# A three-sublayer model on 4096 tokens: projection, scan, router and first mixture as one pipeline over blocks of 512 tokens

## The reference, cut to what matters

```python
# scan, per sequence; x_in = x @ w_in, (dt_low, B, C) = split(x_in @ w_x)
dt = softplus(dt_low @ w_dt + b_dt) * (DT_MAX - DT_MIN) + DT_MIN
A = -exp(A_log)                       # 128 channels x 16 states
def step(h, inp):
    dA = dtt[:, :, None] * A
    h = exp(dA) * h + einsum('bdn,bn,bd->bn', dA, bt, ut)[:, None, :]
    y = einsum('bdn,bn->bd', h, ct) + Dp * ut
# mixture over N = 4096 tokens, 8 experts, capacity C = 512
logits = x @ Wr + br
probs = softmax(logits); gate = max(probs); idx = argmax(probs)
mask = one_hot(idx); pos = cumsum(mask, axis=0) * mask
mask = mask * (pos < C)               # the tokens behind the 511th of an expert are dropped
gate = gate * sum(mask)
combine = gate * one_hot(idx) x one_hot(pos)
expert_in = einsum('nd,nec->ecd', x, combine)
h = relu(expert_in @ W1[e] + b1[e]); eo = h @ W2[e] + b2[e]
out = einsum('ecd,nec->nd', eo, combine)
```

## Time and profile before

| | us |
|---|---|
| median of 3 runs | 571.65 |
| span of the profiled execution | 585.5 |
| PE busy | 312.8 |
| DVE busy | 362.3 |
| ACT busy | 224.5 |
| POOL busy | 306.3 |

### The profile page before, as it was taken

One profiled execution on the slowest core, in us unless ns is written; L12 is line 12 of the kernel. 1 busy time (PEld: TensorE's weight loads), 2 busy tenths in 40 slices (PEclk: granted clock), 3 DMA queues, 4 the chain that ended last, 5 costly groups with the idle time before them and its releaser, 6 DMA issues.

```text
span 585.5 us, 5360 instructions
## 1 busy us (share of the span) xinstructions
PE 312.8 (53%) x1281; PEld 160.1 (27%) x1281; DVE 362.3 (62%) x801; ACT 224.5 (38%) x350; POOL 306.3 (52%) x225
## 2 busy tenths in 40 slices
PE   4878343666657657565150826054787464073700
PEld 3333110111111112145140513022575453042400
DVE  4484689999999999976250202195689964011204
ACT  2768854355354354214140302056546022120303
POOL 3041155777686677745655366337224855627550
PEclk9988775787787787875555868559989575567655
DMA  7003429500000000020104421430000000143019
GB/s 194 0 1 107 161 58 319 219 0 1 0 0 0 0 0 0 0 57 27 50 33 123 134 81 40 118 93 1 1 1 6 32 33 28 50 137 107 36 66 266
DMA packets 34996, 37.74 MB, mean 64 GB/s; under 512 B 5529, under 2 KB 27035, under 8 KB 34972
## 3 DMA queue, kind: packets, MB, share of 16 engines
q1 hardware_dynamic: 30076, 28.34, 16.4%
q0 software_dynamic: 4096, 8.43, 4.0%
q10 hardware_dynamic: 800, 0.71, 0.4%
HBM read 17.47 MB, written 19.99 MB: 64 GB/s over the span
## 4 chain that ended last, share of the span: by engine, by line
issue 34%; PE 6%; POOL 4%; another core or an unknown queue 4%; SPq 3%; DMA 3%; ACT 1%; DVE 0%; POOLq 0%; ACTq 0%; DVEq 0%
POOL answers L1063 4%; PE ps L989 2%; PE ps L998 2%; DMA back<-answers 1%; PE ps L980 1%; SPq L1147 1%; SPq L1080 1%; SPq L949 1%; DMA rows<-slots 1%; DMA answers<-reply,home 1%; ACT rows_t L1018 0%; ACT back L1089 0%; ACT hidden L1024 0%; DVE reply L1052 0%
## 5 line engine op out<-in xcount | busy, mean ns | idle before, releaser
L643 POOL TENSOR_TENSOR states<-states,c_rows 128x1024 f32<-128x1024 f32 x44 | 119.1, 2709 | 51.0 <-DVE states L663 50.8
L663 DVE TENSOR_TENSOR_SCAN states<-ps,inp 128x1024 f32<-128x1024 f32 x64 | 142.2, 2268 | 2.6 <-ACT ps L628 2.6
L628 ACT ACTIVATE ps<-ps,bias_p,scale_p 128x1024 f32<-128x1024 f32 x64 | 74.4, 1176 | 88.4 <-PE ps L566 88.4
L1063 POOL DMA_INDIRECT answers<-reply,home x64 | 61.4, 959 | 51.3 <-DVE reply L1052 33.3
L566 PE MATMUL ps<-stack,sel 96*128 (+1 forms) x128 | 49.3, 486 | 69.2 <-DVE states L663 63.2
L890 POOL DMA_INDIRECT slots<-gated,put x64 | 63.5, 993 | 42.4 <-ACT gated L882 24.7
L1052 DVE TENSOR_TENSOR reply<-ps,b 128x512 f32 x16 | 11.1, 691 | 67.3 <-PE ps L998 45.3
L577 PE MATMUL ps<-states,red 128*32 128x512 f32 x256 | 46.0, 813 | 2.3 <-POOL states L643 2.3
L566 PEld LDWEIGHTS ps<-stack,sel 96*128 96x128 bf16 x128 | 9.0, 104 | 122.3 <-DVE states L663 89.1
L733 POOL TENSOR_TENSOR rstd<-spread,neg_half 128x8 f32<-128x8 f32 x12 | 20.8, 1736 | 32.1 <-DVE neg_mean L727 32.1
L989 PE MATMUL ps<-rows_t,e_w 128*128 128x512 f32 x32 | 23.1, 812 | 19.2 <-ACT rows_t L1018 19.2
(11 more groups left out here) (160 smaller groups left out, 607.2 us busy)
## 6 DMA issues: line engine op xcount, KB each, us to landing
slots<-zero SPq DMA_DIRECT2D x8, 516.0 KB
rows<-slots SPq DMA_DIRECT2D x16, 258.0 KB, 2.7
back<-answers SPq DMA_DIRECT2D x8, 512.0 KB, 6.1
steps<-part SPq DMA_DIRECT2D x4, 768.0 KB, 3.2
stack<-steps SPq DMA_DIRECT2D x12, 256.0 KB, 4.0
x<-in_x SPq DMA_DIRECT2D x4, 512.0 KB, 5.8
answers<-zero SPq DMA_DIRECT2D x4, 512.0 KB
e_w<-in_f_W SPq DMA_DIRECT2D x16, 128.0 KB
```

Of the source, the lines that this page charges most:

```text
L628: act.activation(slot(u), slot(u), ACT.Exp, scale=m["scale_p"][:, group(u):group(u) + 1], bias=m["bias_p"][:, group(u):group(u) + 1]).then ...
L643: eng.tensor_tensor(h[:, u * SEQ:(u + 1) * SEQ], h[:, u * SEQ:(u + 1) * SEQ], c_rows[:, bass.ds(b * SEQ, SEQ)], ALU.mult).then_inc(done, 1)
L663: dve.tensor_tensor_scan(h[:, u * SEQ:(u + 1) * SEQ], slot(u), inp[:, bass.ds(b * SEQ, SEQ)], 0.0, ALU.mult, ALU.add).then_inc(scanned, 1)
L1063: pool.indirect_dma_start(out=m["answers"], out_offset=bass.IndirectOffsetOnAxis(m["home"][:, e, j:j + 1], 0), in_=m["reply"][:, e, j * D: ...
```

## The change

Both plans stay, but the first now holds everything up to the first mixture in one function, `stream`, and the second (`conv_and_mixture`) starts with the statistics for the convolution. The unit is a block of 512 tokens (8 blocks); the scan of a sequence's second block starts from the last states of the first. All engines run through one list of steps, 16 steps (channel groups) to a block, and each piece of work has a fixed place in it: the constants give the step, counted from the block's first scan, at which a piece is issued. Buffers for two blocks take the place of those for all sequences; the scan's buffer in PSUM becomes three single banks.

The layer norm moves: the mean is taken out by the matrix `center` folded into the weights, and the normalization for the router is applied to the logits. The residual x and the scan's output are summed in PSUM (`state_sum`), go out transposed (`xt`), back to tokens (`back`, `take_x`), and feed the logits. All products with C are on POOL.

The first mixture computes all 8 experts for all tokens: a first layer (`first`) from the transposed block, and a second bf16 matmul onto it, from 56 features per token, which adds the bias and a term of -1e30 for each expert that wasn't chosen, so that its Relu gives zero; the second layers (`second`) of all experts sum up in one bank, and `mix` adds the result, weighted by gate and capacity, into x. The weight of expert layers stays in SBUF for the second mixture. The convolution's filter and its weights are prepared inside the steps (`prepare`, steps 1 to 20). The first block's step sizes are broadcast by fp32 matmuls, without the way over DRAM. The second mixture is as before, with its two loops written out. `need` now issues no wait where the count is zero.

```diff
-            project(plan, ps, m, t)
-            scan(plan, ps, m, t)
+            stream(plan, ps, m, t)
...
+DECAY, Y_BANK, TURN_BANK, PROJ_BANK, HIDDEN_BANK, OUT_BANK = 0, 3, 4, 5, 6, 7
+AHEAD = 2
+LAG = 3
+RING = 12
+STATS_IN, POW_IN, NORMAL_IN, TOKENS_IN = -20, -19, -18, -17
+Z_AT, U_AT, B_AT, C_AT, Q_AT = -16, -15, -14, -13, -11
+SOFTPLUS, DTU, HIGH, REST, MIDDLE, LOW, INPUT = -13, -12, -12, -11, -10, -9, -10
+SUMS = QUARTERS - 1 + LAG
+TAKE_Y, BACK, TAKE_X, LOGITS, STATS_X, POW_X, CHOOSE, PROB, COUNT, PLACE, FEATURES, WEIGH = 19, 19, 20, 20, 21, 22, 23, 24, 24, 25, 26, 27
+MIX = 27
+FIRST_STEP, LAST_STEP = STATS_IN, GROUPS * (BLOCKS - 1) + MIX + 2 * EXPERTS + 3
...
+        def clear(dst, b):
+            wide = dst.shape[1]
+            sp.dma_start(dst[b * SEQ:(b + 1) * SEQ, :].rearrange("(p j) d -> p (j d)", p=P), zero[:, 0:BT * wide]).then_inc(prepared, 16)
+        def spread_steps(k):
+            need(sp, low_done, k)
+            sp.dma_start(m["steps"][:, k * PARTS * HALF:(k + 1) * PARTS * HALF], part[:, :, :].rearrange("p a s -> p (a s)")).then_inc(steps_out, 16)
+            sp.wait_ge(steps_out, k * 16)
+            need(sp, dt_psum, GROUPS * (k - 1))
+            for a in range(PARTS):
+                sp.dma_start(stack[a * QUARTER:(a + 1) * QUARTER, k % 2, :, :],
+                             m["steps"][:, (k * PARTS + a) * HALF:(k * PARTS + a + 1) * HALF].rearrange("(q r) s -> r q s", r=QUARTER)
+                             ).then_inc(stacked[k], 16)
...
+        for k in range(2, BLOCKS):
+            if k + 2 < BLOCKS:
+                load_x(k + 2)
+            spread_steps(k)
+            if 2 <= k < 2 + BATCH:
+                clear(m["slots"], k - 2)
+                clear(m["answers"][TOKENS:, :], k - 2)
+        sp.wait_ge(prepared, 16 * (2 + 2 * BATCH))
...
+        def broadcast(n):
+            k, g = n // GROUPS, group(n % GROUPS)
+            need(pe, scanned, n - 2)
+            at = bank(ps, DECAY + n % 3)
+            if k == 0:
+                pe.wait_ge(dts_done, 1)
+                pe.wait_ge(sel_made, 1)
+                pe.matmul(at, sel_whole[:, n * P:(n + 1) * P], dts[:, 0, :], start=True, stop=True).then_inc(dt_psum, 1)
+            else:
+                if n % GROUPS == 0:
+                    pe.wait_ge(stacked[k], 16 * PARTS)
+                pe.matmul(at, sel[0:PARTS * QUARTER, (g % QG) * P:(g % QG + 1) * P], stack[:, k % 2, g // QG, :], start=True,
+                          stop=True).then_inc(dt_psum, 1)
+                need(pe, y_taken, k)
+                pe.matmul(bank(ps, Y_BANK), diag[:, :], u_t[:, k % 2, :], start=True, stop=False)
+                for i in range(HT):
+                    pe.matmul(ps[:, Y_BANK * HALF + i * P:Y_BANK * HALF + (i + 1) * P], x[:, tile(k, i)], ident, start=False, stop=False)
+            need(pe, product_done, GROUPS * k + QUARTERS * (r + 1))
+            for c in range(QUARTERS):
+                last = pe.matmul(ps[c * QUARTER:(c + 1) * QUARTER, Y_BANK * HALF:(Y_BANK + 1) * HALF],
+                                 red[:, r * QUARTER:(r + 1) * QUARTER], made[:, (GROUPS * k + QUARTERS * r + c) % RING, :],
+                                 start=False, stop=r == QG - 1)
+            last.then_inc(summed, 1)
...
+        def back(k):
+            pe.wait_ge(y_taken, k + 1)
+            need(pe, *turn.free("back", k))
+            for i in range(HT):
+                last = pe.transpose(ps[:, TURN_BANK * HALF + i * P:TURN_BANK * HALF + (i + 1) * P], xt[:, k % 2, i * P:(i + 1) * P], ident)
+            last.then_inc(turn.full, 1)
+        def logits(k):
+            pe.wait_ge(prep_done, 1)
+            need(pe, *turn.free("logits", k))
+            for i in range(HT):
+                last = pe.matmul(ps[:, TURN_BANK * HALF + i * EXPERTS:TURN_BANK * HALF + (i + 1) * EXPERTS], xt[:, k % 2, i * P:(i + 1) * P],
+                                 m["w_r"][:, :], start=True, stop=True)
+            last.then_inc(turn.full, 1)
...
+        def features(k):
+            pe.wait_ge(feats_done, k + 1)
+            need(pe, *turn.free("features", k))
+            for i in range(HT):
+                last = pe.matmul(ps[0:FEATS, TURN_BANK * HALF + i * P:TURN_BANK * HALF + (i + 1) * P],
+                                 feats[:, i, :, :].rearrange("p s e -> p (s e)"), m["ident_bf"][:, :], start=True, stop=True)
+            last.then_inc(turn.full, 1)
+        def first(k, e):
+            if e == 0:
+                pe.wait_ge(prep_done, 6)
+                need(pe, *turn.gone("features", k))
+            need(pe, hidden_done, EXPERTS * k + e)
+            pe.matmul(bank(ps, HIDDEN_BANK), m["w1"][:, e, :], xt[:, k % 2, :], start=True, stop=False)
+            pe.matmul(bank(ps, HIDDEN_BANK), opened_t[:, e, :], feats_t[:, k % 2, :], start=False, stop=True).then_inc(hidden_psum, 1)
+        def second(k, e):
+            if e == 0:
+                need(pe, mixed, k)
+                for i in range(HT):
+                    pe.matmul(ps[:, OUT_BANK * HALF + i * D:OUT_BANK * HALF + (i + 1) * D], feats_t[:, k % 2, i * P:(i + 1) * P], added_t[:, :],
+                              start=i == 0, stop=False)
+            pe.wait_ge(hidden_done, EXPERTS * k + e + 1)
+            for i in range(HT):
+                last = pe.matmul(ps[:, OUT_BANK * HALF + i * D:OUT_BANK * HALF + (i + 1) * D], hidden[:, e % 2, i * P:(i + 1) * P],
+                                 m["w2"][:, e, :], start=False, stop=(e, i) == (EXPERTS - 1, HT - 1))
+            last.then_inc(out_psum, 1)
...
+        for s in range(FIRST_STEP, LAST_STEP):
+            if 0 <= s + AHEAD < GROUPS * BLOCKS:
+                broadcast(s + AHEAD)
+            for r in range(QG):
+                for k in due(s, SUMS + QUARTERS * r):
...
+        def decay(n):
+            g = group(n % GROUPS)
+            act.wait_ge(dt_psum, n + 1)
+            if n == 0:
+                act.wait_ge(scale_made, 1)
+            at = bank(ps, DECAY + n % 3)
+            act.activation(at, at, ACT.Exp, scale=scale_p[:, g:g + 1]).then_inc(decay_ready, 1)
+        def normalize(k):
+            act.wait_ge(rstd_done, k + 1)
+            need(act, turn.full, turn.at("tokens", k - 1))
+            for i in range(HT):
+                last = act.activation(xn[:, i * D:(i + 1) * D], x[:, tile(k, i)], ACT.Copy, scale=rstd[:, i:i + 1])
+            last.then_inc(xn_ready, 1)
+        def take_tokens(k):
+            need(act, turn.full, turn.at("tokens", k))
+            need(act, proj.full, proj.at("c", k - 1))
...
+        def take_u(k):
+            need(act, proj.full, proj.at("u", k))
+            need(act, summed, QG * (k - 2) + 1)
+            need(act, dtu_done, k - 1)
+            act.copy(u_t[:, k % 2, :], bank(ps, PROJ_BANK)).then_inc(proj.left["scalar"], 1)
+        def take_y(k):
+            need(act, summed, QG * (k + 1))
+            need(act, hidden_psum, EXPERTS * (k - 1))
+            act.copy(xt[:, k % 2, :], bank(ps, Y_BANK)).then_inc(y_taken, 1)
+        def take_x(k):
+            need(act, turn.full, turn.at("back", k))
+            act.copy(x[:, block_cols(k)], bank(ps, TURN_BANK)).then_inc(turn.left["scalar"], 1)
...
+        def take_features(k):
+            need(act, turn.full, turn.at("features", k))
+            need(act, out_psum, EXPERTS * (k - 1))
+        def hide(k, e):
+            act.wait_ge(hidden_psum, EXPERTS * k + e + 1)
+            need(act, out_psum, EXPERTS * k + e - 1)
+            act.activation(hidden[:, e % 2, :], bank(ps, HIDDEN_BANK), ACT.Relu).then_inc(hidden_done, 1)
...
+        def step_times_u(k):
+            dve.drain()
+            need(dve, *proj.gone("u", k))
+            need(dve, proj.full, proj.at("q", k - 1))
+            dve.tensor_tensor(dtu[:, :], dts[:, k % 2, :], u_t[:, k % 2, :], ALU.mult).then_inc(dtu_done, 1)
+        def scan(n):
+            k, u = divmod(n, GROUPS)
+            if u == 0:
+                dve.drain()
+            dve.wait_ge(decay_ready, n + 1)
+            need(dve, product_done, n - GROUPS + 1)
+            initial = states[:, u, HALF - 1:HALF] if k % 2 else 0.0
+            dve.tensor_tensor_scan(states[:, u, :], bank(ps, DECAY + n % 3), inp[:, k % 2, :], initial, ALU.mult, ALU.add).then_inc(scanned, 1)
...
+        def weigh(k):
+            need(dve, turn.full, turn.at("counts", k))
+            dve.tensor_tensor(cum[:, :, :], turn_rows, onehot, ALU.mult).then_inc(turn.left["vector"], 1)
+            dve.drain()
+            dve.tensor_reduce(pos[:, :], cum[:, :, :], AX, ALU.add)
+            dve.drain()
+            dve.scalar_tensor_tensor(out=weight[:, k % 2, :], in0=pos[:, :], scalar=float(CAP), in1=gain[:, :], op0=ALU.is_lt,
+                                     op1=ALU.mult).then_inc(weight_done, 1)
+        def mix(k):
+            need(dve, out_psum, EXPERTS * (k + 1))
+            dve.wait_ge(weight_done, k + 1)
+            for i in range(HT):
```

(22 more changed lines are left out.)

1436 lines of the change are left out of this document (713 added, 723 removed).

## The result

The changed kernel takes 618.33 us (median of 4 runs, 616.18 to 621.78) beside 571.66 for the kernel before (4 runs, 570.14 to 572.26): ratio 1.083, 95% interval 1.079 to 1.087. In a second set on another occasion it took 619.69 beside 571.15: 1.082 (1.076 to 1.087). Forecast were 568 us, with a range of 536 to 606. The profiled execution was the slowest of the four (621.78 us, span 619.9).

A forecast was written before the change was run, and what follows sets the result against it. PE's list of 35.0 us a block was taken as the bound, 41.5 with waits and meetings; (a) to (e) end at 380, the whole span at 582.5, less the profile's excess of 13.9 gives 568 us, range 536 to 606.

The forecast's parts named there:

- (a): Start of the kernel until the first scan, from folded weights through block 1's statistics: 23 us.
- (b): Steps 0 to 15, without mixture but with fp32 broadcasts, block 1's projection, the filter and weights: 31 us.
- (c): Steps 16 to 26, with block 0's router but no mixture: 24 us.
- (d): Steady state from step 27, projection, scan, router and mixture together: 101 steps at 41.5 us a block, 262 us.
- (e): After the last scan: router chain 18, eight experts 18.4, last hidden, output and mix 3.5; 40 us.
- switch, statistics, first normalization: Between the first mixture and the convolution: new Plan 2.7 us, statistics to normalization 4.9.
- span to median: The old profiled span lay 13.9 us above the median; this was carried over from 582.5 to 568.
- PE's list: PE's summed work per steady-state block at the high clock: 35.0 us, the largest of all engines.
- Rival 4: Clock falls in router steps, half the work at 1.2 GHz: block 52, 635 us; chance 0.12 together with rival 5.
- The waits: PE's waits per block: transposes back 1.3 us, logits 1.9, features behind weigh about 1.9.
- The meetings: DVE held up by POOL's products: 0 to 4.4 us a block on DVE, 1.0 taken on PE's path.
- Rival 3: DVE loses every meeting with POOL, 4.4 us a block instead of 1.0: block 45, 590 us; chance 0.08.

The follow-up runs named there:

- two different experiments: Changed kernel with POOL's products cut to 16 columns from the 13th on: 599.1 us; changed kernel with products waiting for DVE's operations: 604.2 us.
- quiet products: Changed kernel with POOL's product waiting until DVE's softplus, step times u, choose, place or weigh of the same step is done: 604.2 us, ratio 1.059.
- edits of order: Router's power before POOL's product, block 1's statistics earlier, filter's gates a step later; measured only with the other mends on the changed kernel: 555.2 us, 0.972.
- spread steps: Changed kernel with other step numbers only, so PE never needs what ACT or DVE does in the same step: 593.0 us, ratio 1.036.
- warm start: Discarded matmuls added around the folded weights, first projections and broadcasts of steps 3 to 31, on spread steps: 591.4 us, where before took 591.9.
- second profile of after: The changed kernel run and profiled again without any edit: 619.7 us, ratio 1.082.
- best kernel: Changed kernel with spread steps, POOL's waiting products, discarded matmuls before and among the first projections, and three edits of order: 555.2 us, ratio 0.972.
- second profile of before: The kernel before, unchanged, profiled again: span 570.9 us, time 572.75.

## Why the prediction was wrong

By its own steps, with what the profile after shows (us):

| term | forecast | measured | difference |
|---|---|---|---|
| (a) until the first scan | 23 | 30.6 | +7.6 |
| (b) steps 0 to 15 | 31 | 37.0 | +6.0 |
| (c) steps 16 to 26 | 24 | 35.1 | +11.1 |
| (d) steps 27 to the last | 262 | 279.6 | +17.6 |
| (e) after the last scan | 40 | 39.4 | -0.6 |
| switch, statistics, first normalization | 7.6 | 5.1 | -2.5 |
| from there to the end | 194.9 | 193.1 | -1.8 |
| span to median | -14.5 | -1.6 | +12.9 |
| sum | 568.0 | 618.3 | +50.3 |

The measured (d) runs from scan 27 to the start of scan 127, 100 steps, where the forecast counted 101; the last step stands in (e). Step for step (d) is 20 us too long (279.6 against 259.4).

**The step that failed** in (d) is the clock: "In the steady state PE is 84% busy with wide matmuls and its longest wait is 2 us, so I take the high clock." PE was 85% busy, but the longest wait was 3.5 us, not 2, and the granted clock was 0.89, just under the 0.9 that the prediction had named as its own refutation. Term by term of (d): PE's list of 35.0 a block is 219 us over the 100 steps. With the waits gone and the clock at 0.98 PE is busy 215 to 216 in the same stretch: the list was right. At 0.89 it is busy 239: +20, the whole of what (d) is too long. PE's idle time is 40.5, against 5.5 + 1.0 a block = 41: right in sum. What was missed is that the idle stretches are paid twice, once as waiting and once as slow matmuls after them. Rival 4 named the clock, but as a fall for half of the work, with a price of 10 us a block; it was 3.

**The waits.** Priced at 1.3 + 1.9 + 1.9, measured 1.2 + 1.9 + 2.9. Forecast as a fixed tax, they were a choice of step numbers: moving them took 29 us from scans 27 to 127, of which PE's busy time gives 17 and its idle time 12.

**The meetings** of DVE and POOL were mis-sized: "I take 1.0", against 1.9 a block by two different experiments, part of it by way of the clock (0.92 instead of 0.89). Rival 3 was nearly right on what DVE loses (4.0 a block, for 4.4) and wrong in putting all of it on the block. The prediction had held back because in the earlier trace rows POOL's product was the one that lengthened (3.14). The Trainium skill (SBUF — State Buffer, section "SBUF: two separate sides") gives an exclusive lock that also covers operations with two SBUF inputs. The runs side with it: factor, on 4 elements, 0.95 us beside products and 0.16 without. The meetings reach TensorE through the router's chain: with quiet products its wait for weigh falls from 14.6 to 8.6 us between 100 and 330 us.

**The start (a to c), +24.7,** is half of the miss and got the least thought. (a) took the high level for the first products; they took 2.05 each, and with discarded matmuls before them the first scan came at 24.1. (b) left out that DVE waits in its list for the filter's exponentials (3.1 us) and PE for block 1's normalization (2.2), which stands behind a power that stands behind block 0: with the edits of order, the spread steps and the warm start (b) takes 32.0 instead of 37.0 (35.4 in the second profile of after), and 29.9 with quiet products too (forecast 31). They were not tried one by one. (c) remains 5.6 above its 24 in the best kernel, at a clock of 0.83 (0.74 in the changed kernel); how much of it is the clock isn't shown.

**The base.** 12.9 us of the miss are that the span of before was 13.9 above its median in one profile, and the forecast carried this over as if it belonged to every profile (the working has 14.5, because 582.5 less 13.9 is 568.6 and it says 568). It belonged to that execution: 10.8 of the 14.6 us by which the two spans of before differ lie in the first router and mixture, the very stages that the change removes. Against the second profile of before the forecast's own sum, a span of 582.5, is 11.6 slower than before: the working as a whole said slower, and the base turned it round. The unrolled second mixture had no -4 to give either, since 3.8 of that were the hole of the first profile: the tail from the first normalization is 195.6 in the second profile of before and 193.1 after.

Right were the lists of PE, the length of (e), the mixture's end on PE, and the place of each of the three waits. DVE's list of 30.4 a block is 29.2 with quiet products. ACT's 26 was too much: it is busy 21.5 a block, 48% instead of 60%.

## What to carry to other kernels

A pipeline whose bound is TensorE pays for an idle stretch twice, so first ask of every in-order engine which result of its own step it waits for, and shift that one step: numbers in a table gave 25 of the 47 us back. Before a stage is removed, profile the kernel twice: a time that only one execution shows lies perhaps just there. Between DVE and GpSimd let the longer operation wait for the short dependent ones; a semaphore that exists already was enough.

## What the runs showed of the hardware

- With less work for TensorE the kernel was slower: four experts against eight, block 46.3 against 44.7, and 43.2 against 40.1 with spread steps, at granted clocks of 0.73 and 0.77. The cause isn't isolated.
- In a stretch where TensorE was 85% busy the granted clock still fell twice in the block looked at, to 0.62 and 0.57 in windows of 4 us, behind a wait of 2.40 us and behind two of 1.16 and 1.86.
- In the first 30 us the granted clock reads 1.00 while 512-column fp32 products take 2.05 us, near the 1.91 of a first layer at 201.3 us, in a window at 0.50, which is the 1.2 GHz level. So a 1.00 in the first microseconds doesn't say that the high level holds; the durations do. After 60 discarded small matmuls, and 8 more ahead of each, they took 1.08 to 1.10.
- A DVE operation on 4 elements per partition took 0.95 us on average beside products on GpSimd, 0.16 without.
